# A fused attention and feed-forward layer on eight cores: the weights' fp32-to-bf16 conversion is moved from VectorE into the GpSimd-issued load

## The chip, the cores and the metric

The kernel runs on all 8 cores of one Trainium2 chip. Each core takes two of the sixteen sequences of the batch and all the weights; nothing is exchanged between cores. The metric is the device time in microseconds of the slowest core.

## What is computed

```
x = L0_attn_x                                  # 16 x 2048 x 1024, fp32
h = layernorm(x)
keys    = h @ triu(Wk).T                       # 16 heads of 64
queries = h @ tril(Wq).T
values  = h @ Wv.T
att = softmax(queries . keys / 8)              # per head, 2048 x 2048
x = x + layernorm((att . values) @ Wu.T + bu)
g = layernorm(x)
x = x + layernorm(g @ weight.T + pooled(g) @ disha)   # pooled: sum over 16 groups of 64 columns
```

Each layernorm is over the 1024 columns, with epsilon 1e-5 and no gain. All matrix products are done in bf16 with fp32 accumulation.

## The kernel before

One core works through its two sequences, b = 0 and b = 1, of 2048 rows each (16 blocks of 128 rows). There are five 1024x1024 fp32 weights in HBM. TensorE wants them in bf16 and transposed, so each is brought in by eight *preps*, one for each block of 128 rows (`prep_weight_thunks`, L232). A prep has these steps:

- SyncE (SP) issues the load of the fp32 rows into one of two staging tiles `wraw0`, `wraw1` (L245). A full block is 128x1024, 512 KB.
- VectorE casts them to the single bf16 tile `wc2` (L249).
- For Wk and Wq, which are triangular, only 1 to 8 of the 128-column groups are loaded. SP loads a 128x128 mask into the single tile `mkt0` (L253) and VectorE multiplies the diagonal group by it (L257).
- TensorE transposes each 128x128 group by a matmul with the identity into the PSUM tile `psO` (L262). Below, the up to 8 matmuls of one prep are called T.
- VectorE (in the first stage ScalarE) evacuates `psO` to the resident weight tile `slotA`, `slotB` or `slotC` (L278, L273).

`mini_prep_thunk` (L284) does the same for the first row block of Wk and of Wq into a tile `mini`, with L286 the load, L289 the cast, L293 and L296 the mask, L300 the transposes and L305 the evacuation.

Every engine runs its instructions in the order in which the Python code emits them. A small class `Prog` keeps, for each named region, the last writer and the readers since, and turns these into semaphore waits. A DMA is an instruction of the queue of the engine that issues it, and a waiting instruction holds up all behind it on that engine. A load into a tile waits for the last reader of what stood there.

The stages are, in order of time:

1. `ph1`, b = 0 only (0 to 176 us): layernorm and transposition of the 16 row blocks, with the 24 preps of Wk, Wq and Wv mixed in, three (Wk, Wq, Wv) in each of the first eight steps, and the first projections.
2. `ph2` (176 to 1025 us for b = 0, 1341 to 2150 us for b = 1): attention in 32 *units*. A unit is two heads by 512 queries, with 16 steps of two score matmuls (L499, L505), one exponential of 128x1024 on ScalarE (L511) and two matmuls with the values (L522, L528). The score matmuls of the next step are emitted ahead of the current step's value matmuls. At the end of each unit `emit_tail` (L535) inverts the row sums on ScalarE (L541, L543), sends them over HBM to be spread over 64 partitions (`rrd`, `rbsb`; L546, L548, L552), multiplies on VectorE (L557, L561), and moves one half to the upper partitions (L565). These four DMAs are issued by GpSimd (POOL). Behind the tails of units 26, 27, 28 and 29 stand four preps each, eight of Wu and then eight of the feed-forward weight. That is the case in both passes over `ph2`. Units 13 to 28 of b = 0 also carry the row statistics of b = 1 (`stats_thunks`), and the two mini preps stand behind the tail of unit 31 of b = 0.
3. `ph34` (1025 to 1297 us, 2150 to 2388 us): output projection, layernorms, feed-forward product and stores, as a software pipeline over the 16 row blocks. POOL issues its stores `xp` and `out` (L713, L776), SP its loads. At its end, for b = 0, stand the 16 preps of Wk and Wq for b = 1 (1297 to 1341 us).

So before, POOL's queue holds only the tails' DMAs and the stores, and all weight loads are on SP's queue, where the two staging tiles let it run up to two preps ahead.

Of the kernel before, what the change touches and what calls it, by code (L numbers as in the profile page):

```python
# [6 lines left out]
F32 = mybir.dt.float32  # L7
BF16 = mybir.dt.bfloat16
# [131 lines left out]
D = 1024  # L140
# [10 lines left out]
def build_nc():  # L151
# [16 lines left out]
    sb = lambda n, sh, dt: es.enter_context(nc.sbuf_tensor(n, sh, dt))  # L168
# [26 lines left out]
    onescf = sb("onescf", [1, 128], F32)  # L195
    ones128 = sb("ones128", [128, 1], BF16)
    idn = sb("idn_s", [128, 128], BF16)
    wraw = [sb("wraw0", [128, D], F32), sb("wraw1", [128, D], F32)]
    wc2 = sb("wc2", [128, D], BF16)
    mkt = [sb("mkt0", [128, D], BF16)] * 2  # L200
    dstg = jnk

    def make_fam(pfx):
# [7 lines left out]
    def fk(fam, n, j):  # L211
# [3 lines left out]
    psO = pst("psO")  # L215
# [3 lines left out]
    p = Prog()  # L219
# [6 lines left out]
         writes=["bub"], tag="bu_b16")  # L226
# [5 lines left out]
    def prep_weight_thunks(wd, slot_t, slot_key, mask_d, tagp, tri=None,  # L232
                           widx=0, evac_eng="dve"):
        ths = []
        for fb in range(NDC):
            def th(fb=fb):
                if tri == "low":
                    lo, hi = 0, fb + 1
                elif tri == "up":
                    lo, hi = fb, NDC  # L240
                else:
                    lo, hi = 0, NDC
                wr = wraw[(fb + widx) % 2]
                wrk = f"wraw{(fb + widx) % 2}"
                p.dma("sync", lambda e: e.dma_start(  # L245
                    wr[:, lo * 128:hi * 128],
                    wd[fb * 128:(fb + 1) * 128, lo * 128:hi * 128]),
                    writes=[wrk], tag=f"{tagp}_ld{fb}")
                p.op("dve", lambda e: e.tensor_copy(  # L249
                    wc2[:, lo * 128:hi * 128], wr[:, lo * 128:hi * 128]),  # L250
                    reads=[wrk], writes=["wc2"], tag=f"{tagp}_c{fb}")
                if mask_d is not None:
                    p.dma("sync", lambda e: e.dma_start(  # L253
                        mkt[0][:, 0:128],
                        mask_d[fb * 128:(fb + 1) * 128, fb * 128:(fb + 1) * 128]),
                        writes=["mkt0"], tag=f"{tagp}_ldm{fb}")
                    p.op("dve", lambda e: e.tensor_mul(  # L257
                        wc2[:, fb * 128:(fb + 1) * 128],
                        wc2[:, fb * 128:(fb + 1) * 128], mkt[0][:, 0:128]),
                        reads=["mkt0", "wc2"], writes=["wc2"], tag=f"{tagp}_m{fb}")  # L260
                for dc in range(lo, hi):
                    p.op("pe", lambda e, dc=dc: e.matmul(  # L262
                        psO[:, dc * 128:(dc + 1) * 128],
                        wc2[:, dc * 128:(dc + 1) * 128],
                        idn[:], start=True, stop=True),
                        reads=["wc2", "idn"], writes=["psO"],
                        tag=f"{tagp}_t{fb}_{dc}")
                sdst = lambda: slot_t[:].rearrange(
                    "p (dc f) -> p dc f", dc=NDC)[:, lo:hi, fb * 128:(fb + 1) * 128]
                ssrc = lambda: psO[:, :].rearrange(  # L270
                    "p (dc f) -> p dc f", dc=NDC)[:, lo:hi, :]
                if evac_eng == "act":
                    p.op("act", lambda e: e.activation(  # L273
                        sdst(), ssrc(), AF.Identity),
                        reads=["psO"], writes=[(slot_key, fb)],
                        tag=f"{tagp}_e{fb}")
                else:
                    p.op("dve", lambda e: e.tensor_copy(sdst(), ssrc()),  # L278
                         reads=["psO"], writes=[(slot_key, fb)],
                         tag=f"{tagp}_e{fb}")  # L280
            ths.append(th)
        return ths

    def mini_prep_thunk(wd, mask_d, base, mkey, tagp, ndc=NDC):  # L284
        def th():
            p.dma("sync", lambda e: e.dma_start(  # L286
                wraw[0][:, 0:ndc * 128], wd[0:128, 0:ndc * 128]),
                writes=["wraw0"], tag=f"{tagp}_ld")
            p.op("dve", lambda e: e.tensor_copy(  # L289
                wc2[:, 0:ndc * 128], wraw[0][:, 0:ndc * 128]),  # L290
                reads=["wraw0"], writes=["wc2"], tag=f"{tagp}_c")
            if mask_d is not None:
                p.dma("sync", lambda e: e.dma_start(  # L293
                    mkt[0][:, 0:128], mask_d[0:128, 0:128]), writes=["mkt0"],
                    tag=f"{tagp}_lm")
                p.op("dve", lambda e: e.tensor_mul(  # L296
                    wc2[:, 0:128], wc2[:, 0:128], mkt[0][:, 0:128]),
                    reads=["mkt0", "wc2"], writes=["wc2"], tag=f"{tagp}_m")
            for dc in range(ndc):
                p.op("pe", lambda e, dc=dc: e.matmul(  # L300
                    psO[:, dc * 128:(dc + 1) * 128],
                    wc2[:, dc * 128:(dc + 1) * 128],
                    idn[:], start=True, stop=True),
                    reads=["wc2", "idn"], writes=["psO"], tag=f"{tagp}_t{dc}")
            p.op("dve", lambda e: e.tensor_copy(  # L305
                mini[:, base:base + ndc * 128], psO[:, 0:ndc * 128]),
                reads=["psO"], writes=[mkey], tag=f"{tagp}_e")
        return th
# [629 lines left out]
```

How the kernel before makes its waits and increments, by code:

```python
                    def body(eng):  # L111
                        highwater = {}
                        for o in self.ops[eng_name]:
                            needed = {}
                            for prod in o.waits:
                                if prod not in sem_val_after:
                                    raise RuntimeError(
                                        f"dep of {o.tag} on {prod.tag} lost")
                                k, v = sem_val_after[prod]
                                if needed.get(k, 0) < v:
                                    needed[k] = v
                            for k, v in needed.items():
                                if highwater.get(k, 0) < v:
                                    eng.wait_ge(sems[k], v)
                                    highwater[k] = v
                            inst = o.fn(eng)
                            if o in sem_val_after:
                                k, _ = sem_val_after[o]
                                inst.then_inc(sems[k], 16 if o.is_dma else 1)
                        for k, v in counters.items():
                            if highwater.get(k, 0) < v:
                                eng.wait_ge(sems[k], v)
```

## Time and profile before

| | us |
|---|---|
| median of 2 runs | 2366.76 (2365.36 to 2368.15) |
| the profiled execution | 2389.16 |
| its span, core 0, the slowest | 2387.6 |
| spans of the eight cores | 2353.2 to 2387.6 |
| busy in the span: PE, ACT, DVE, POOL | 1705.7, 1502.0, 663.6, 167.5 |

The span runs from the first to the last instruction of the slowest core. PE is TensorE, ACT ScalarE, DVE VectorE, POOL GpSimd, SP SyncE. A POOL or SP row of a DMA is its issue; its data land later. The number in square brackets of a row is the time the engine sat idle before it, with what ended the wait. "x8" is a count of like instructions that were merged in one row.

### The profile page before, as it was taken

The page shows a single profiled execution, that of the slowest core. Times are in us where ns is not written, and L with a number is a line of the kernel's source. Part 1 is how long each engine was busy: PE and PEld are TensorE (multiplying, and loading weights), DVE is VectorE, ACT ScalarE, POOL GpSimd, SP SyncE. Part 2 cuts the span into 40 slices and gives each one's busy share as a digit, 9 for nine tenths or more (in the row PEclk, how much of TensorE's full clock was granted, in tenths as well). Part 3 has the DMA queues.
Part 4 walks back from the last instruction along what each step waited for, and adds up shares of the span by engine and source line. Part 5 has one row for each costly group of instructions (what it writes and reads, how often), then busy time and mean ns, then how long its engine had stood idle before and what let it go on. Part 6 is the DMA issues. An engine that isn't in the chain of part 4 may idle for free.

```text
span 2387.6 us, 28615 instructions; the slowest of 8 cores (2353.2 to 2387.6 us)
## 1 busy us (share of the span) xinstructions
PE 1705.7 (71%) x8793; PEld 625.6 (26%) x8793; DVE 663.6 (28%) x1515; ACT 1502.0 (63%) x1821; POOL 167.5 (7%) x324
## 2 busy tenths in 40 slices
PE   1358888888888654667774588888888884557773
PEld 1232322322323221123332132322322222112231
DVE  3441111122223231224454211111111113123544
ACT  3347777777778644536663377777787873555554
POOL 0000010000000100000000001010000100000000
PEclk9769877779989877778886699999899896779887
DMA  3320000000111021125554200000000002112443
GB/s 115 127 95 12 12 16 13 15 23 30 44 34 48 18 93 54 34 95 174 166 179 141 69 13 17 12 18 12 18 16 13 18 12 81 42 55 86 151 166 141
DMA packets 51590, 148.04 MB, mean 62 GB/s; under 512 B 14193, under 2 KB 15857, under 8 KB 51442
## 3 DMA queue, kind: packets, MB, share of 16 engines
q1 hardware_dynamic: 31986, 91.41, 12.0%
q0 software_dynamic: 19456, 54.81, 6.5%
q8 instruction: 75, 1.23, 0.2%
q14 instruction: 73, 0.60, 0.1%
HBM read 108.17 MB, written 33.82 MB: 59 GB/s over the span
## 4 chain that ended last, share of the span: by engine, by line
PE 48%; ACT 21%; issue 13%; DVE 11%; DMA 5%; ACTq 1%; DVEq 0%; SPq 0%; POOLq 0%; POOL 0%
ACT pt L511 11%; PE psS L499 11%; PE psO L522 5%; PE psM L522 5%; PE psO L528 4%; PE psM L423 4%; PE psM L528 4%; PE psM L454 3%; PE psO L423 3%; PE psO L454 3%; ACT fbuf L541 2%; PE psS L664 2%; PE psS L736 2%; PE psO L262 2%; DVE qf L438 2%
## 5 line engine op out<-in xcount | busy, mean ns | idle before, releaser
L511 ACT ACTIVATE pt<-psS 128x1024 bf16<-128x1024 f32 x1024 | 1031.8, 1024 | 514.8 <-PE psS L505 413.2
L505 PE MATMUL psS<-qf,kf 64*128 64x512 bf16 x1024 | 436.3, 426 | 0.0
L499 PE MATMUL psS<-qf,kf 64*128 64x512 bf16 x1024 | 436.3, 426 | 0.0
L522 PE MATMUL psO<-pt,vp 128*65 128x512 bf16 x512 | 221.2, 432 | 101.6 <-ACT pt L511 95.6
L522 PE MATMUL psM<-pt,vp 128*65 128x512 bf16 x512 | 214.3, 419 | 107.8 <-ACT pt L511 105.5
L262 PE MATMUL psO<-idn_s,wc 128*128 128x128 bf16 x464 | 60.9, 305 | 246.4 <-DVE wc L249 147.0
L499 PEld LDWEIGHTS psS<-qf,kf 64*128 64x128 bf16 x1024 | 95.8, 94 | 490.8 <-issue 490.7
L528 PE MATMUL psO<-pt,vp 128*65 128x512 bf16 x512 | 220.3, 430 | 0.0
L736 PE MATMUL psS<-slotB,lnxt 128*128 128x512 bf16 x512 | 156.5, 474 | 85.5 <-ACT lnxt L367 84.2
L528 PE MATMUL psM<-pt,vp 128*65 128x512 bf16 x512 | 213.5, 417 | 0.0
L664 PE MATMUL psS<-slotA,aofm 128*128 128x512 bf16 x512 | 127.4, 394 | 16.7 <-ACT psS L687 11.5
L546 POOL DMA_DIRECT2D rrd<-fbuf x64 | 32.3, 504 | 1392.0 <-ACT fbuf L543 1392.0
L557 DVE TENSOR_TENSOR aofm<-psO,rbsb 64x512 bf16<-64x512 f32 x32 | 21.9, 683 | 355.4 <-DMA rbsb<-rrd 299.6
L454 PE MATMUL psM<-slotC,lnxt 128*128 128x128 bf16 x1152 | 97.4, 232 | 31.1 <-DVE kf L438 17.8
L522 PEld LDWEIGHTS psO<-pt,vp 128*65 128x65 bf16 x512 | 59.2, 116 | 209.9 <-issue 202.5
L522 PEld LDWEIGHTS psM<-pt,vp 128*65 128x65 bf16 x512 | 58.4, 114 | 211.0 <-issue 203.6
L262 PEld LDWEIGHTS psO<-idn_s,wc 128*128 128x128 bf16 x464 | 44.1, 135 | 264.6 <-issue 264.6
L557 DVE TENSOR_TENSOR aofm<-psM,rbsb 64x512 bf16<-64x512 f32 x32 | 21.9, 683 | 324.8 <-DMA rbsb<-rrd 254.4
L736 PEld LDWEIGHTS psS<-slotB,lnxt 128*128 128x128 bf16 x512 | 57.7, 117 | 174.5 <-issue 145.2
L505 PEld LDWEIGHTS psS<-qf,kf 64*128 64x128 bf16 x1024 | 95.9, 94 | 0.0
L465 DVE CAST vp<-psM 128x128 bf16<-128x128 f32 x144 | 42.3, 294 | 177.2 <-PE psM L454 168.2
L454 PEld LDWEIGHTS psM<-slotC,lnxt 128*128 128x128 bf16 x1152 | 72.2, 104 | 63.2 <-issue 63.2
(114 smaller groups left out, 1878.4 us busy)
## 6 DMA issues: line engine op xcount, KB each, us to landing
xt<-x SPq DMA_DIRECT2D x64, 512.0 KB, 4.2
rbsb<-rrd POOLq DMA_DIRECT2D x128, 128.0 KB, 2.9
xp<-xt POOLq DMA_DIRECT2D x32, 512.0 KB, 3.5
xt<-xp SPq DMA_DIRECT2D x32, 512.0 KB, 3.6
out<-xt POOLq DMA_DIRECT2D x32, 512.0 KB, 2.9
wraw<-wu SPq DMA_DIRECT2D x16, 512.0 KB, 4.2
wraw<-wf SPq DMA_DIRECT2D x16, 512.0 KB, 4.1
fbuf<-x SPq DMA_DIRECT2D x16, 512.0 KB, 5.3
```

What stands on the lines that cost most here:

```text
L262: p.op("pe", lambda e, dc=dc: e.matmul(psO[:, dc * 128:(dc + 1) * 128], wc2[:, dc * 128:(dc + 1) * 128], idn[:], start=True, stop=True), r ...
L423: slot_t=slot_t, half=half: e.matmul(ps[:, qtr * 512:(qtr + 1) * 512], slot_t[:, colf(dc):colf(dc) + 128], lnxt[:, dc * T + (half * 2 + qt ...
L438: p.op("dve", lambda e: e.tensor_copy(dst_t[:, (half * 2 + qtr) * 512:(half * 2 + qtr) * 512 + 512], ps[:, qtr * 512:(qtr + 1) * 512]), re ...
L454: p.op("pe", lambda e, tcl=tcl, tc=tc, dc=dc, ps=ps: e.matmul(ps[:, tcl * 128:(tcl + 1) * 128], lnxt[:, dc * T + tc * 128:dc * T + (tc + 1 ...
L499: p.op("pe", lambda e: e.matmul(psS[sp][:, 0:512], kf[par][0:64, kc * 128:(kc + 1) * 128], qf[par][0:64, q0:q0 + 512], start=True, stop=Tr ...
L505: p.op("pe", lambda e: e.matmul(psS[sp][:, 512:1024], kf[par][64:128, kc * 128:(kc + 1) * 128], qf[par][64:128, q0:q0 + 512], start=True, ...
L511: p.op("act", lambda e: e.activation(pt[sp][:, :], psS[sp][:, :], AF.Exp, scale=SCALE), reads=[PSS[sp]], writes=[f"pt{sp}"], tag=f"u{uidx} ...
L522: p.op("pe", lambda e: e.matmul(psA[0:65, 0:512], vp[par][:, kc * 130:kc * 130 + 65], pt[sp][:, 0:512], start=(kc == 0), stop=(kc == KCN - 1),
L528: p.op("pe", lambda e: e.matmul(psA[0:65, 512:1024], vp[par][:, kc * 130 + 65:kc * 130 + 130], pt[sp][:, 512:1024], start=(kc == 0), stop= ...
L541: p.op("act", lambda e: e.activation(fbuf[0][64:65, :], psA[64:65, :], AF.Ln), reads=[psk], writes=["fbuf0"], tag=f"u{uidx}rc1")
L664: p.op("pe", lambda e, half=half, ec=ec: e.matmul(psS[0][:, half * 512:(half + 1) * 512], aofm[:, ec * T + tc * 128:ec * T + (tc + 1) * 12 ...
L736: p.op("pe", lambda e, half=half, dc=dc: e.matmul(psS[1][:, half * 512:(half + 1) * 512], lnxt[:, dc * T + tc * 128:dc * T + (tc + 1) * 12 ...
```

## The change

The fp32 staging tiles and the cast are taken away. POOL issues the weight load straight into a bf16 tile, and the DMA converts from fp32 to bf16. There are now two bf16 tiles (`wc2a`, `wc2b`), used in turn, and two mask tiles, used in turn. The mini preps use the first tile of each kind only. The masks stay on SP's queue. The row blocks, the matmuls, the evacuations and the order of all on PE and ACT are the same. A line number of after is 1 to 4 lower than that of before for the same statement.

```diff
-    wraw = [sb("wraw0", [128, D], F32), sb("wraw1", [128, D], F32)]
-    wc2 = sb("wc2", [128, D], BF16)
-    mkt = [sb("mkt0", [128, D], BF16)] * 2
+    wcp = [sb("wc2a", [128, D], BF16), sb("wc2b", [128, D], BF16)]
+    wc2 = wcp[0]
+    mkt = [sb("mkt0", [128, 128], BF16), sb("mkt1", [128, 128], BF16)]
...
-                wr = wraw[(fb + widx) % 2]
-                wrk = f"wraw{(fb + widx) % 2}"
-                p.dma("sync", lambda e: e.dma_start(
-                    wr[:, lo * 128:hi * 128],
+                wi = (fb + widx) % 2
+                wc = wcp[wi]
+                wck = f"wc2{wi}"
+                p.dma("pool", lambda e: e.dma_start(
+                    wc[:, lo * 128:hi * 128],
                     wd[fb * 128:(fb + 1) * 128, lo * 128:hi * 128]),
-                    writes=[wrk], tag=f"{tagp}_ld{fb}")
-                p.op("dve", lambda e: e.tensor_copy(
-                    wc2[:, lo * 128:hi * 128], wr[:, lo * 128:hi * 128]),
-                    reads=[wrk], writes=["wc2"], tag=f"{tagp}_c{fb}")
+                    writes=[wck], tag=f"{tagp}_ld{fb}")
...
     def mini_prep_thunk(wd, mask_d, base, mkey, tagp, ndc=NDC):
         def th():
-            p.dma("sync", lambda e: e.dma_start(
-                wraw[0][:, 0:ndc * 128], wd[0:128, 0:ndc * 128]),
-                writes=["wraw0"], tag=f"{tagp}_ld")
-            p.op("dve", lambda e: e.tensor_copy(
-                wc2[:, 0:ndc * 128], wraw[0][:, 0:ndc * 128]),
-                reads=["wraw0"], writes=["wc2"], tag=f"{tagp}_c")
+            p.dma("pool", lambda e: e.dma_start(
+                wc2[:, 0:ndc * 128], wd[0:128, 0:ndc * 128]),
+                writes=["wc20"], tag=f"{tagp}_ld")
```

The mask multiply, the transposes and the mask load follow the tile by its key (`wck`, `mkt{wi}`).

What this does to the order shows best at the end of a unit that has preps. Before, POOL's queue at the end of unit 26 of b = 0 is the tail's four DMAs (`rrd`, `rbsb` twice, `aofm`), and then the next unit's:

```order
L546 DMA rrd<-fbuf0 16x1x64
L548 DMA rbsb<-rrd 64x512
L552 DMA rbsb<-rrd 64x512
L565 DMA aofm<-stg2 64x512
L546 DMA rrd<-fbuf0 16x1x64
```

After, the four loads of Wu's row blocks stand between the two:

```order
L542 DMA rrd<-fbuf0 16x1x64
L544 DMA rbsb<-rrd 64x512
L548 DMA rbsb<-rrd 64x512
L561 DMA aofm<-stg2 64x512
L246 DMA wc2a<-wu 128x1024
L246 DMA wc2b<-wu 128x1024
L246 DMA wc2a<-wu 128x1024
L246 DMA wc2b<-wu 128x1024
L542 DMA rrd<-fbuf0 16x1x64
```

The loads have moved from SP's queue, where nothing but other weight loads and the statistics' `xt` loads stood ahead of them, to behind `aofm<-stg2`.

On VectorE the same place reads, before, with the casts between the tail's two multiplies (L557, L561), the evacuations to `slotA` and the statistics (L577, L580):

```order
L557 TENSOR_TENSOR aofm<-psO,rbsb 64x512
L561 TENSOR_TENSOR stg2<-psO,rbsb 64x512
L249 CAST wc2<-wraw0 128x1024
L278 CAST slotA<-psO 128x8x128
L249 CAST wc2<-wraw1 128x1024
L278 CAST slotA<-psO 128x8x128
L249 CAST wc2<-wraw0 128x1024
L278 CAST slotA<-psO 128x8x128
L249 CAST wc2<-wraw1 128x1024
L278 CAST slotA<-psO 128x8x128
L577 TENSOR_REDUCE sxal<-xt1 128x1
```

and after:

```order
L553 TENSOR_TENSOR aofm<-psO,rbsb 64x512
L557 TENSOR_TENSOR stg2<-psO,rbsb 64x512
L277 CAST slotA<-psO 128x8x128 x4
L573 TENSOR_REDUCE sxal<-xt1 128x1
L576 SCALAR_TENSOR_TENSOR jnk,sqal<-xt1 128x1024
```

The casts are gone and nothing takes their place. The third place is POOL's queue at the end of unit 31 of b = 0, ahead of the first stores `xp` of `ph34`. After, the loads of the two mini preps stand there, both into `wc2a`, behind the tail's last DMA:

```order
L542 DMA rrd<-fbuf0 16x1x64
L544 DMA rbsb<-rrd 64x512
L548 DMA rbsb<-rrd 64x512
L561 DMA aofm<-stg2 64x512
L285 DMA wc2a<-wk 128x1024
L285 DMA wc2a<-wq 128x128
L709 DMA xp<-xt0 128x1024
```

Before, L713, the `xp` store, followed L565 directly there.

## Rows read from the trace of the kernel before

**Rows 1.** The page's costliest groups: the transposes of the preps.
```profile
L262 PE MATMUL psO<-idn_s,wc 128*128 128x128 bf16 x464 | 60.9, 305 | 246.4 <-DVE wc L249 147.0
```
**Rows 2.** Timeline, end of unit 26 of b = 0: start us, us, engine, instruction.
```profile
832.19 0.68 DVE L561 TENSOR_TENSOR stg<-psO,rbsb 64x512 bf16<-64x512 f32 x1
832.79 0.68 DVE L249 CAST wc<-wraw 128x1024 bf16<-128x1024 f32 x1
833.44 0.52 POOL L565 DMA_DIRECT2D aofm<-stg  x1 [4.01 <-DVE stg L561]
...
833.72 1.01 PE L262 MATMUL psO<-idn_s,wc 128*128 128x128 bf16 x8 [10.65 <-DVE wc L249]
834.84 1.23 DVE L278 CAST slotA<-psO 128x1024 bf16<-128x1024 f32 x1 [1.37 <-PE psO L262]
...
842.99 1.01 PE L262 MATMUL psO<-idn_s,wc 128*128 128x128 bf16 x8 [2.08 <-DVE wc L249]
843.93 0.60 PE L499 MATMUL psS<-qf,kf 64*128 64x512 bf16 x1
...
844.66 1.02 ACT L511 ACTIVATE pt<-psS 128x1024 bf16<-128x1024 f32 x1 [19.00 <-PE psS L505]
```
**Rows 3.** Timeline, end of unit 29 of b = 1, the last of the eight.
```profile
2097.54 0.67 DVE L561 TENSOR_TENSOR stg<-psM,rbsb 64x512 bf16<-64x512 f32 x1
...
2109.18 0.60 PE L499 MATMUL psS<-qf,kf 64*128 64x512 bf16 x1
```
**Rows 4.** DMA issues of the whole run: count, KB each, median us to landing.
```profile
out<-xt POOLq DMA_DIRECT2D x32, 512.0 KB, 2.9
wraw<-wu SPq DMA_DIRECT2D x16, 512.0 KB, 4.2
...
aofm<-stg POOLq DMA_DIRECT2D x64, 64.0 KB, 1.9
```
**Rows 5.** Tile wraw, 820 to 1020 us.
```profile
DMA to landing us min/median/max: 3.6/4.6/5.5
```
**Rows 6.** Line L713, the stores xp.
```profile
DMA to landing us min/median/max: 2.9/3.5/7.1
```
**Rows 7.** Tile wraw: the casts, ns min/median/max.
```profile
L249 DVE CAST wc<-wraw x72: 216/680/695, 20.1 to 2107.4; 128x1024 bf16<-128x1024 f32 x44, 128x128 bf16<-128x128 f32 x4, 128x896 bf16<-128x896 f32 x4, 128x256 bf16<-128x256 f32 x4
```
**Rows 8.** Timeline, the first two steps of ph1.
```profile
21.38 1.01 PE L262 MATMUL psO<-idn_s,wc 128*128 128x128 bf16 x8 [21.38 <-DVE wc L257]
21.63 0.38 SPq L245 DMA_DIRECT2D wraw<-wv  x1
...
25.24 0.27 PE L262 MATMUL psO<-idn_s,wc 128*128 128x128 bf16 x1 [2.85 <-DVE wc L257]
...
27.14 1.01 PE L262 MATMUL psO<-idn_s,wc 128*128 128x128 bf16 x8 [1.64 <-DVE wc L249]
...
34.55 0.90 PE L262 MATMUL psO<-idn_s,wc 128*128 128x128 bf16 x7 [2.99 <-DVE wc L257]
...
39.90 1.01 PE L262 MATMUL psO<-idn_s,wc 128*128 128x128 bf16 x8 [1.49 <-DVE wc L249]
```
**Rows 9.** Timeline, the 16 preps between the sequences: the first and the last.
```profile
1289.74 0.53 POOL L776 DMA_DIRECT2D out<-xt  x1 [9.49 <-DVE vp L465]
...
1297.79 0.22 DVE L257 TENSOR_TENSOR wc<-wc,mkt 128x128 bf16<-128x128 bf16 x1
...
1298.16 1.01 PE L262 MATMUL psO<-idn_s,wc 128*128 128x128 bf16 x8 [1.47 <-DVE wc L257]
...
1340.18 1.01 PE L262 MATMUL psO<-idn_s,wc 128*128 128x128 bf16 x8 [2.64 <-DVE wc L257]
```
**Rows 10.** Timeline, the mini preps at the end of unit 31 of b = 0.
```profile
1020.57 0.52 POOL L565 DMA_DIRECT2D aofm<-stg  x1 [3.92 <-DVE stg L561]
...
1021.08 1.01 PE L300 MATMUL psO<-idn_s,wc 128*128 128x128 bf16 x8 [11.35 <-DVE wc L296]
...
1025.31 0.26 PE L300 MATMUL psO<-idn_s,wc 128*128 128x128 bf16 x1 [3.23 <-DVE wc L296]
```

More of the change, by code:

```diff
@@ L242, in th @@
                     lo, hi = 0, NDC
-                wr = wraw[(fb + widx) % 2]
-                wrk = f"wraw{(fb + widx) % 2}"
-                p.dma("sync", lambda e: e.dma_start(
-                    wr[:, lo * 128:hi * 128],
+                wi = (fb + widx) % 2
[3 more added lines that the diff above has]
+                    wc[:, lo * 128:hi * 128],
                     wd[fb * 128:(fb + 1) * 128, lo * 128:hi * 128]),
-                    writes=[wrk], tag=f"{tagp}_ld{fb}")
-                p.op("dve", lambda e: e.tensor_copy(
-                    wc2[:, lo * 128:hi * 128], wr[:, lo * 128:hi * 128]),
-                    reads=[wrk], writes=["wc2"], tag=f"{tagp}_c{fb}")
+                    writes=[wck], tag=f"{tagp}_ld{fb}")
                 if mask_d is not None:
                     p.dma("sync", lambda e: e.dma_start(
-                        mkt[0][:, 0:128],
+                        mkt[wi][:, 0:128],
                         mask_d[fb * 128:(fb + 1) * 128, fb * 128:(fb + 1) * 128]),
-                        writes=["mkt0"], tag=f"{tagp}_ldm{fb}")
+                        writes=[f"mkt{wi}"], tag=f"{tagp}_ldm{fb}")
                     p.op("dve", lambda e: e.tensor_mul(
-                        wc2[:, fb * 128:(fb + 1) * 128],
-                        wc2[:, fb * 128:(fb + 1) * 128], mkt[0][:, 0:128]),
-                        reads=["mkt0", "wc2"], writes=["wc2"], tag=f"{tagp}_m{fb}")
+                        wc[:, fb * 128:(fb + 1) * 128],
+                        wc[:, fb * 128:(fb + 1) * 128], mkt[wi][:, 0:128]),
+                        reads=[f"mkt{wi}", wck], writes=[wck],
+                        tag=f"{tagp}_m{fb}")
                 for dc in range(lo, hi):
@@ L263, in th @@
                         psO[:, dc * 128:(dc + 1) * 128],
-                        wc2[:, dc * 128:(dc + 1) * 128],
+                        wc[:, dc * 128:(dc + 1) * 128],
                         idn[:], start=True, stop=True),
-                        reads=["wc2", "idn"], writes=["psO"],
+                        reads=[wck, "idn"], writes=["psO"],
                         tag=f"{tagp}_t{fb}_{dc}")
@@ L297, in th @@
                     wc2[:, 0:128], wc2[:, 0:128], mkt[0][:, 0:128]),
-                    reads=["mkt0", "wc2"], writes=["wc2"], tag=f"{tagp}_m")
+                    reads=["mkt0", "wc20"], writes=["wc20"], tag=f"{tagp}_m")
             for dc in range(ndc):
@@ L303, in th @@
                     idn[:], start=True, stop=True),
-                    reads=["wc2", "idn"], writes=["psO"], tag=f"{tagp}_t{dc}")
+                    reads=["wc20", "idn"], writes=["psO"], tag=f"{tagp}_t{dc}")
             p.op("dve", lambda e: e.tensor_copy(
```

## The prediction

> **What bounds the kernel now.** I read the page's groups first, for the instructions that the change touches. The transposes of the preps are 61 us of TensorE's work, yet TensorE sat idle 246.4 us before them, and 147.0 us of that ended on the cast [rows 1]. So the preps are made of waits, and the question is what each wait consists of and what comes last once the cast is gone. The timeline answers it, place by place. There are four places.
>
> The first is the end of a unit that carries preps [rows 2]. TensorE takes its work in order, so the score matmul of the next unit (L499) stands behind four T. VectorE ends the tail's last multiply at 832.87 (832.19 + 0.68) and casts at once, because the fp32 rows were already there: SP had loaded them long before. T starts at 833.72, the fourth at 842.99, and L499 at 843.93. ScalarE, which carries the exponentials, was idle 19.00 us. From the multiply's end to L499 it is 11.06 us. At the last of the eight such unit ends it is 2109.18 - 2098.21 = 10.97 us [rows 3]. Nothing covers this time, so each microsecond added or taken here is a microsecond of the span.
>
> The others are the first eight steps of ph1 [rows 8], the 16 preps between the sequences [rows 9], and the two mini preps [rows 10]. The attention units without preps and ph34 proper hold no prep, and I count nothing there.
>
> **The unknown: the converting load.** No row shows a DMA that converts. I call L its time from issue to landing for 512 KB of fp32. The nearest rows are POOL's stores of the same bytes, 2.9 us [rows 4], SP's weight loads over the run, 4.2 [rows 4], SP's weight loads in the stage with the preps, 3.6 to 5.5 with a median of 4.6 [rows 5], and POOL's slowest `xp` store, 7.1 [rows 6]. I take 4.4, between the two medians of loads of the same rows, and keep 2.9 and 7.1 as the ends. For 64 KB I take 2.5, somewhat over POOL's 1.9 for 64 KB within SBUF [rows 4]. By these two points a block of k groups takes 2.23 + 0.27k.
>
> **Unit ends, eight times.** What goes is the cast, 0.68 us, four times. What comes is that the loads stand on POOL behind `aofm<-stg`, which waits for the tail's multiply. The prefetch is lost altogether: the tiles are free, but the queue is not. Count from the multiply's end. POOL starts `aofm<-stg` 0.57 later (833.44 - 832.87) and is done at 1.09. Load 1 lands at 1.09 + L and T1 starts 0.1 later. T1 takes 1.01, its evacuation 1.23 with 0.11 ahead of it, so T2 starts 2.45 after T1 and ends at 4.65 + L. Load 4 goes into the tile that T2 read. It is issued 0.57 later (the same delay of POOL), lands L later, and T4 takes 0.1 + 1.01 more: 6.33 + 2L. Load 3 with T3 and its evacuation lets T4 start at the same time. Against 11.0 before, the difference is 2L - 4.7, which is +4.1 at L = 4.4. Eight times that is **+32.8**. Two load times are exposed where there were none, and the four casts don't pay for them. Break-even is L = 2.35, below every row of this size.
>
> **ph1, eight steps.** The pace of a step is set by Wv: before, SP issues its load 0.25 after T of Wk starts (21.63 against 21.38), since the cast had freed the staging tile. T of Wv starts 5.76 and 5.35 us after T of Wk in the two steps shown [rows 8], 5.55 in the mean. After, that load waits until T of Wk has ended: 0.64 (mean of 1.01 for eight groups and 0.27 for one) + 0.57 + 4.4 + 0.1 = 5.71, so +0.15. The cast of Wk ahead of its T also goes: it lies between 0.68 for eight groups and 0.22 for one, 0.45 in the mean [rows 7]. Net -0.3 a step, **-2.4**. The cast of Wv lay inside the 5.55. The mask wait of Wq goes too, but Wv is later anyway, so it is worth nothing.
>
> **Preps between the sequences.** Before, the first T starts at 1298.16 and the last ends at 1341.19 [rows 9]. POOL's last `out` store is issued at 1289.74, so loads 1 and 2 follow it and have landed before VectorE gets there. The first T starts 0.7 earlier (no cast), at 1297.5, and the second near 1300.1. From there every load waits for the T two before it. A pair costs T 0.64 + 0.57 + load 3.35 (mean of the seven blocks, 4.1 groups) + mask multiply 0.22 and its handovers 0.15, 4.93 in all. Seven pairs are 34.5: the last T starts at 1334.6 and ends at 1335.6, **-5.6**.
>
> **Mini preps.** Before, both were ready at once, T starting at 1021.08 and 1025.31 [rows 10]. After, the load of Wk follows `aofm<-stg` on POOL at 1021.09, so its T starts at 1021.09 + 4.4 + 0.1 + 0.37 = 1025.96, +4.9. The second load goes into the same tile and waits for the first T: 1.01 + 0.57 + 2.5 + 0.47 = 4.55 against 4.23 before, +0.3. Together **+5.2**. The first output projection waits behind them on TensorE.
>
> **Sum.** 32.8 - 2.4 - 5.6 + 5.2 = +30.0 us. The profiled execution took 2389.16 us (span 2387.6), 0.95% over the median of the runs. The unit ends are waits on DMA and VectorE, alike on any core, so I add the same microseconds to the median: 2366.76 + 30.0 = 2396.8, +1.3%. By the profiled execution it is 2419.2. Per microsecond of L the sum moves by 16 + 8 + 7 + 2 = 33 us.
>
> **Rivals.** *The converting load is quick.* At L = 2.9, POOL's time for the same bytes outward, the unit ends cost 1.1 each (+8.8), ph1 gives back 14.4, the preps between the sequences some 14 (there the chain of T, evacuation and multiply then holds), and the minis cost 2.2: 2349 us, -0.7%. For it speaks that POOL's rows are shorter than SP's. Against it, a store is no load from HBM, and two loads are in flight together. The Trainium skill, in "DMA: Bandwidth & Descriptors", section "Anatomy of one DMA — SWDGE (gpsimd) path", gives for a DMA issued from GpSimd a fixed 2.0 us plus its bytes at 436 GB/s. For 512 KB that is an estimate of 3.2 us, and by it the sum would be 9.6 us below before, 2357. This case's `out` row agrees with it roughly, SP's loads do not.
>
> *The converting load is slow.* The conversion is work that no DMA here does yet, and it is exposed twice at each unit end and once in every ph1 step. At L = 7.1 the sum is 8 x 9.5 + 19.2 + 13.3 + 10.6 = +119, 2486 us. The place is the unit end, the price 16 us of the span per microsecond of L there, and from L = 4.9 on the kernel is slower by over 2% (47 us). Against it speaks that the write into SBUF is half as long and POOL's issue takes the 0.52 us of any other. The Trainium skill, in "SBUF — State Buffer", section "SBUF: two separate sides", warns that a DMA issued from GpSimd can stall when VectorE runs a fast-mode copy, as its descriptors can't be written meanwhile. The same change takes those casts away, so by that rule this rival gets weaker; no row here shows such a stall.
>
> *POOL's queue delays the tails or stores.* A load waiting for a T would hold up the next unit's `rrd` store. But the fourth load is issued before T4, and `rrd` comes a whole unit later. The stores of ph34 have no load ahead of them but the minis'. I give it no price and count it in the chances above.
>
> **How the numbers follow.** Forecast 48% (L from 3.8 to 4.9), quick load 20%, slow load 32%. Low end: L = 3.2, 2357. High end: L = 6, 30 + 53 = +83, 2450. Beyond them I leave about a tenth on either side. Faster by over 2%, about what a measurement of this kernel can tell from no change, would need more than all that the quick case gives: 2%. Slower by over 2% is the slow case, 32%. Within 2%: 66%.
>
> **What would show it.** In the profile after: look at the landing time of `wc<-wu` on POOL's queue (4.4), at the time from the tail's multiply to L499 at unit 26 (15.1 instead of 11.06) with ScalarE idle some 23 us, at T of Wv 5.7 us behind T of Wk in ph1, at 38 us instead of 43 for the preps between the sequences, and at the first mini T 5 us later behind the tail's multiply. TensorE's wait before T should end on a DMA where it ended on the cast. I am wrong if the loads at unit ends are issued ahead of `aofm<-stg`, if L is outside 3.8 to 4.9, or if the units without preps change their length.

## The result, and the profile after

After takes 2406.53 us (median of 9 runs, 2402.91 to 2443.79), before 2366.19 (8 runs, 2360.06 to 2400.14). The ratio is 1.0171, with a 95% interval of 1.0157 to 1.0185: slower by 1.7%, clear of the noise but within the 2% that counts as no change. The forecast was 2396.8, +30.0 us; measured it is +40.3. Some executions of either kernel fall into a slower state, in which one die is granted a lower clock (the 2443.79 is one), and every ratio here leaves those out.

First the page's groups of after: the transposes of the preps, now one group for each bf16 tile.

```profile
L261 PE MATMUL psO<-idn_s,wc2a 128*128 128x128 bf16 x236 | 30.9, 306 | 211.6 <-DMA wc2a<-wu 75.4
L261 PE MATMUL psO<-idn_s,wc2b 128*128 128x128 bf16 x228 | 30.0, 305 | 72.6 <-DMA wc2b<-wv 18.1
```

TensorE's work is the same 61 us. Its idle time before them has grown from 246.4 us [rows 1] to 284.2, and it ends on a DMA where it ended on VectorE's cast. VectorE's busy time fell from 663.6 to 625.7 us. The 38 us fewer of VectorE's work did not shorten the program.

The timeline at the end of unit 26 of b = 0, core 3, to be laid beside [rows 2]:

```profile
802.55 1.05 ACT L539 ACTIVATE fbuf<-fbuf 1x1024 f32<-1x1024 f32 x1
807.08 0.50 POOL L542 DMA_DIRECT2D rrd<-fbuf  x1 [17.96 <-issue]
...
813.96 0.67 DVE L557 TENSOR_TENSOR stg<-psO,rbsb 64x512 bf16<-64x512 f32 x1
815.20 0.52 POOL L561 DMA_DIRECT2D aofm<-stg  x1 [4.88 <-DVE stg L557]
815.71 0.57 POOL L246 DMA_DIRECT2D wc2a<-wu  x1
816.27 0.56 POOL L246 DMA_DIRECT2D wc2b<-wu  x1
820.15 1.01 PE L261 MATMUL psO<-idn_s,wc2a 128*128 128x128 bf16 x8 [19.14 <-DMA wc2a<-wu]
...
821.70 0.53 POOL L246 DMA_DIRECT2D wc2a<-wu  x1 [4.87 <-PE psO L261]
822.64 1.01 PE L261 MATMUL psO<-idn_s,wc2b 128*128 128x128 bf16 x8 [1.48 <-DVE slotA L277]
824.19 0.53 POOL L246 DMA_DIRECT2D wc2b<-wu  x1 [1.96 <-PE psO L261]
825.88 1.01 PE L261 MATMUL psO<-idn_s,wc2a 128*128 128x128 bf16 x8 [2.23 <-DMA wc2a<-wu]
828.39 1.01 PE L261 MATMUL psO<-idn_s,wc2b 128*128 128x128 bf16 x8 [1.50 <-DVE slotA L277]
829.34 0.60 PE L495 MATMUL psS<-qf,kf 64*128 64x512 bf16 x1
...
830.07 1.02 ACT L507 ACTIVATE pt<-psS 128x1024 bf16<-128x1024 f32 x1 [26.47 <-PE psS L501]
```

Read it from the multiply's end, 814.63. The loads stand behind `aofm<-stg`. The first T waits for a load, the third T waits for another, and the score matmul L495 comes 14.71 us after the multiply, where it came 11.06 us after it in before. There is one thing more, in the first two rows, that nothing in the forecast had. ACT ends L539 at 803.60, and POOL issues `rrd` 3.48 us later, after 17.96 us of idle time that ended on nothing the profile shows. Over the eight unit ends the time from the multiply to the score matmul is 14.7 to 15.3 us (medians over the cores), where before has 11.0 to 11.3.

The DMA issues of after. The KB are those written, so 256.0 stands for 512 KB read; the last number is the median from issue to landing:

```profile
wc2a<-wu POOLq DMA_DIRECT2D x8, 256.0 KB, 4.0
wc2b<-wu POOLq DMA_DIRECT2D x8, 256.0 KB, 4.5
...
wc2a<-wv POOLq DMA_DIRECT2D x4, 256.0 KB, 4.3
wc2b<-wv POOLq DMA_DIRECT2D x4, 256.0 KB, 5.1
```

In [rows 4] SP's fp32 load of `wu` took 4.2. In the stage with the preps, 820 to 1020 us, line L246 of after shows:

```profile
DMA to landing us min/median/max: 3.7/4.1/4.8
```

Rows say where a wait is, not how much it adds up to. So here is the time by stage, from the trace's records: for each core from the start of one exponential of ScalarE, or one T, to that of the next stage, and then the median over the eight cores of the profiled execution. (`ph34` of b = 1 and the mini preps are counted from the end of the last exponential ahead of them, the minis up to the end of their last T.) Medians don't add up exactly, and `ph1` with the same code came out between 175.6 and 178.9 in three kernels, so a difference of 3 us there says nothing.

| us | before | after |
|---|---|---|
| `ph1` | 175.2 | 175.6 |
| unit end 26, b = 0 | 41.3 | 48.3 |
| the other seven unit ends with preps | 287.2 | 312.8 |
| mini preps | 15.7 | 24.7 |
| preps between the sequences | 41.7 | 42.1 |
| `ph34` of b = 1, to the end | 239.2 | 234.8 |
| of that, last `out` issue to the end | 10.09 | 6.62 |
| whole span | 2355.4 | 2397.6 |

The stage of a unit end is the unit behind it: from its first exponential, which still runs ahead of the T, to the first one of the next unit. The units without preps agree within 1 us per 13 units. So the loss is at the unit ends, +32.6, and at the minis, +9.0. `ph1` and the preps between the sequences have gained nothing. The end of the program has given back 3.5.

The minis, core 3, against [rows 10]:

```profile
1018.03 0.52 POOL L561 DMA_DIRECT2D aofm<-stg  x1 [3.97 <-DVE stg L557]
1018.54 0.57 POOL L285 DMA_DIRECT2D wc2a<-wk  x1
...
1024.13 1.01 PE L296 MATMUL psO<-idn_s,wc2a 128*128 128x128 bf16 x8 [16.46 <-DVE wc2a L292]
1024.49 1.31 SPq L692 DMA_DIRECT2D xt<-x  x3
...
1025.70 0.54 POOL L285 DMA_DIRECT2D wc2a<-wq  x1 [6.58 <-PE psO L296]
1025.96 0.33 SPq L779 DMA_DIRECT2D fbuf<-x  x1
1032.13 0.23 DVE L292 TENSOR_TENSOR wc2a<-wc2a,mkt 128x128 bf16<-128x128 bf16 x1 [5.66 <-DMA wc2a<-wq]
```

The second load writes only 32 KB, and yet the multiply that waits for it comes 6.43 us after its issue. Beside it run four 512 KB loads that SP has just issued (L692, three of them, and L779).

### The profile page after: what moved, and what is told of

Same layout as the page of the kernel before. It is cut to its first block, busy times and chain, and to the rows that moved or that the text cites. A ratio compares the mean times of both kernels' runs of the same rounds, so it can differ in the third digit from the quotient of the medians.

```text
span 2405.5 us, 28454 instructions; the slowest of 8 cores (2387.3 to 2405.5 us)
## 1 busy us (share of the span) xinstructions
PE 1673.4 (70%) x8793; PEld 621.8 (26%) x8793; DVE 625.7 (26%) x1441; ACT 1496.8 (62%) x1821; POOL 206.3 (9%) x398
## 4 chain that ended last, share of the span: by engine, by line
PE 45%; ACT 22%; issue 13%; DVE 10%; DMA 8%; ACTq 1%; DVEq 0%; POOL 0%; POOLq 0%; SPq 0%
ACT pt L507 12%; PE psS L495 10%; PE psO L518 5%; PE psM L518 5%; PE psM L419 4%; PE psO L524 4%; PE psM L524 3%; PE psM L450 3%; PE psO L419 3%; ACT fbuf L537 3%; PE psO L450 2%; PE psS L660 2%; PE psO L261 2%; DVE qf L434 2%; PE psS L732 2%
## 5 line engine op out<-in xcount | busy, mean ns | idle before, releaser
L495 PE MATMUL psS<-qf,kf 64*128 64x512 bf16 x1024 | 425.8, 416 | 0.0
L501 PE MATMUL psS<-qf,kf 64*128 64x512 bf16 x1024 | 425.8, 416 | 0.0
L518 PE MATMUL psO<-pt,vp 128*65 128x512 bf16 x512 | 213.4, 417 | 108.5 <-ACT pt L507 101.9
L518 PE MATMUL psM<-pt,vp 128*65 128x512 bf16 x512 | 209.8, 410 | 108.7 <-ACT pt L507 105.1
L495 PEld LDWEIGHTS psS<-qf,kf 64*128 64x128 bf16 x1024 | 95.4, 93 | 472.0 <-issue 472.0
L524 PE MATMUL psO<-pt,vp 128*65 128x512 bf16 x512 | 212.4, 415 | 0.0
L524 PE MATMUL psM<-pt,vp 128*65 128x512 bf16 x512 | 209.7, 410 | 0.0
L261 PE MATMUL psO<-idn_s,wc2a 128*128 128x128 bf16 x236 | 30.9, 306 | 211.6 <-DMA wc2a<-wu 75.4
L261 PE MATMUL psO<-idn_s,wc2b 128*128 128x128 bf16 x228 | 30.0, 305 | 72.6 <-DMA wc2b<-wv 18.1
## 6 DMA issues: line engine op xcount, KB each, us to landing
wc2a<-wu POOLq DMA_DIRECT2D x8, 256.0 KB, 4.0
```

Of the source, the lines that this page charges most:

```text
L261: p.op("pe", lambda e, dc=dc: e.matmul(psO[:, dc * 128:(dc + 1) * 128], wc[:, dc * 128:(dc + 1) * 128], idn[:], start=True, stop=True), re ...
L495: p.op("pe", lambda e: e.matmul(psS[sp][:, 0:512], kf[par][0:64, kc * 128:(kc + 1) * 128], qf[par][0:64, q0:q0 + 512], start=True, stop=Tr ...
L501: p.op("pe", lambda e: e.matmul(psS[sp][:, 512:1024], kf[par][64:128, kc * 128:(kc + 1) * 128], qf[par][64:128, q0:q0 + 512], start=True, ...
L518: p.op("pe", lambda e: e.matmul(psA[0:65, 0:512], vp[par][:, kc * 130:kc * 130 + 65], pt[sp][:, 0:512], start=(kc == 0), stop=(kc == KCN - 1),
L524: p.op("pe", lambda e: e.matmul(psA[0:65, 512:1024], vp[par][:, kc * 130 + 65:kc * 130 + 130], pt[sp][:, 512:1024], start=(kc == 0), stop= ...
```

## The experiments

**One, the queue without the conversion.** Before, with its fp32 tiles and its casts, but the weight loads issued by POOL:

```diff
-                p.dma("sync", lambda e: e.dma_start(
+                p.dma("pool", lambda e: e.dma_start(
                     wr[:, lo * 128:hi * 128],
...
-            p.dma("sync", lambda e: e.dma_start(
+            p.dma("pool", lambda e: e.dma_start(
                 wraw[0][:, 0:ndc * 128], wd[0:128, 0:ndc * 128]),
```

> The kernel before, with nothing changed but the queue that issues the fp32 weight loads: GpSimd instead of SyncE. VectorE still casts. Theory (the lost prefetch): at each of the eight unit ends the first load is issued only behind aofm<-stg, 1.09 us after the tail's multiply, so the first T starts one load time later; the later loads are released by the casts and hide behind the chain of evacuation, cast and T. Unit ends 1.1 + 4.1 = 5.2 us longer each, 42 us in all, the mini preps some 6 us longer, ph1 and the preps between the sequences within 2 us of before: about 2414 us. Rival (the conversion in the DMA is what is slow, and the queue position costs little): a POOL load of fp32 lands like SP's and the unit ends stay within 1 us of before: 2366 to 2376 us.

Measured: 2424.19 us, ratio 1.0247 (1.0225 to 1.0269). The unit ends cost +43.8 us against before, where 42 was expected. `ph1` cost +7.3 and the preps between the sequences +5.0, where at most 2 was expected for each; those two mostly explain the 10 us by which the kernel is slower than foreseen. Nothing converts here, and the kernel is slower than after. Its loads, by the DMA issues of the run:

```profile
wraw<-wu POOLq DMA_DIRECT2D x16, 512.0 KB, 4.1
...
wraw<-wv POOLq DMA_DIRECT2D x8, 512.0 KB, 5.2
```

Laid beside the rows of after, they show that the conversion costs little or nothing: 4.1 without it, 4.0 and 4.5 with it. (The converting load also writes half the bytes, so a small cost of the conversion and a small gain by the bytes could hide each other; no run tells them apart.) What costs at the unit ends is the place in POOL's queue. In `ph1`, where `wv` is on the path, POOL's loads of it take 5.2 without the conversion and 4.3 and 5.1 with it (after), and SP's 4.0 in the fourth experiment. Why POOL's are longer there isn't shown.

**Two, the prefetch restored.** After, with the first two loads of each group of four issued four steps ahead of the unit's end, before the tail's DMAs:

```diff
+            if kc == KCN - 4:
+                due = [th for mu, th in bpreps if mu <= uidx
+                       and hasattr(th, "pre")][:2]
+                for th in due:
+                    th.pre()
             emit_av(b, uidx, kc)
```

> The changed kernel, with the first two loads of each group of four preps issued four steps ahead of the end of the unit, in front of the tail's DMAs in GpSimd's queue. Theory (the lost prefetch): the first two T start as soon as the tail's multiply lets them, loads 3 and 4 are each exposed in part only, and the multiply-to-L499 time is about 9.4 us after even units and 8.8 after odd ones, where before had 11.0 and the changed kernel about 14.7 to 15: some 48 us less than the changed kernel, about 2358 us. Rival (the converting load is slow by itself): loads 3 and 4 still cost a full load time each beyond that and only half of the 33 us comes back, about 2390 us.

Measured: 2356.56 us, ratio 0.9955 (0.9940 to 0.9970). The unit ends are 16.5 us below before in sum, where after was 32.6 above. The timeline of unit 26 of b = 0, core 4:

```profile
788.72 0.52 POOL L574 DMA_DIRECT2D aofm<-stg  x1 [4.01 <-PE psS L514]
792.16 0.57 POOL L249 DMA_DIRECT2D wc2a<-wu  x1 [2.92 <-PE psS L514]
...
810.26 0.68 DVE L570 TENSOR_TENSOR stg<-psO,rbsb 64x512 bf16<-64x512 f32 x1 [0.31 <-DMA rbsb<-rrd]
811.09 1.01 PE L268 MATMUL psO<-idn_s,wc2a 128*128 128x128 bf16 x8 [10.19 <-DVE stg L570]
...
812.65 0.57 POOL L249 DMA_DIRECT2D wc2a<-wu  x1 [0.62 <-PE psO L268]
...
816.86 1.01 PE L268 MATMUL psO<-idn_s,wc2a 128*128 128x128 bf16 x8 [2.27 <-DMA wc2a<-wu]
...
820.75 0.60 PE L508 MATMUL psS<-qf,kf 64*128 64x512 bf16 x1
```

T1 now waits for the tail's multiply and starts 0.15 us behind it. One load is still exposed, the one before T3. L508 comes 9.81 us after the multiply, below the 11.06 of before. So with the casts gone and half of the prefetch kept the change is a small gain. The rows also put the wait of 2.92 us that ends at 792.16 on POOL. The profile names a matmul as its end, but that had been done for long; experiment seven says what it is.

**Three, more tiles in place of an earlier issue.** After, with four bf16 tiles used in turn and nothing moved:

```diff
-    wcp = [sb("wc2a", [128, D], BF16), sb("wc2b", [128, D], BF16)]
+    wcp = [sb(f"wc2{c}", [128, D], BF16) for c in "abcd"]
...
-                wi = (fb + widx) % 2
+                wi = rot[0] % 4
+                rot[0] += 1
```

> The changed kernel with four bf16 weight tiles used in turn instead of two, nothing moved. Theory: no load waits for a T any more, except in the minis. Unit ends still wait for the first load behind aofm<-stg but for one load only: 13.7 us instead of about 15, 12 us less over the eight. In ph1 the load of Wv is issued before T of Wk and steps get 2 us shorter, 16 in all; the preps between the sequences become a chain of T and evacuation and lose about 10. About 2368 us. Rival (the converting loads are bound by the rate at which they convert): four in flight each take longer, the unit ends and ph1 stay as they are, 2400 us or more.

Measured: 2367.79 us, ratio 1.0003 (0.9981 to 1.0026). The sum comes out as expected, but less of it from the unit ends: they are still 24.1 us above before, 8.5 better than after where 12 was expected. `ph1` went from 175.6 to 153.5 and the preps between the sequences from 42.1 to 33.0. At a unit end the first load is exposed whatever the depth, and with four loads in flight each takes longer from issue to landing than the one before it:

```profile
wc2a<-wu POOLq DMA_DIRECT2D x4, 256.0 KB, 4.0
...
wc2d<-wu POOLq DMA_DIRECT2D x4, 256.0 KB, 6.6
```

**Four, the masks alone.** Before, with nothing changed but the second mask tile:

```diff
-    mkt = [sb("mkt0", [128, D], BF16)] * 2
+    mkt = [sb("mkt0", [128, 128], BF16), sb("mkt1", [128, 128], BF16)]
...
+                mi = (fb + widx) % 2
```

> The kernel before, with nothing of the change but its two mask tiles instead of one. Theory: in the preps between the sequences VectorE waited 8.4 us in nine waits for a mask; these go, so that stage takes 33 us instead of 42, and nothing else moves, since in ph1 the mask wait lies beside the load of Wv: 2358 us. If so, the converting loads cost that stage what the masks gave it. Rival: the masks are hidden there too behind the chain of evacuations, and the time stays 2366 us.

Measured: 2355.24 us, ratio 0.9967 (0.9937 to 0.9997). `ph1` 168.2 instead of 175.2, where nothing was expected; the preps between the sequences 36.6 instead of 41.7, where 9 us less was expected (the 8.4 us of waits for a mask were core 0's; over the cores it is 4.7 to 8.7). The rest is as before. The timeline of the first step of `ph1`, core 0, beside [rows 8], which is the same core:

```profile
18.65 0.33 SPq L246 DMA_DIRECT2D wraw<-wv  x1
...
19.15 1.01 PE L263 MATMUL psO<-idn_s,wc 128*128 128x128 bf16 x8 [19.15 <-DVE wc L258]
...
23.24 1.01 PE L263 MATMUL psO<-idn_s,wc 128*128 128x128 bf16 x8 [1.54 <-DVE wc L250]
```

T of Wv comes 4.09 us behind T of Wk instead of 5.76. In before, Wv's load stood on SP's queue behind the mask's load, which waited for the multiply that used the only mask tile. With two mask tiles Wv's load leaves right after the cast, at 18.65.

So the change was two changes, a queue and a second mask tile. In `ph1` the masks alone give 7.0 us and the queue alone takes 7.3 (experiment one), and after has +0.4. That looks like a sum and isn't one. Once Wv's load is on POOL's queue, no mask stands ahead of it any more. In experiment one, core 2, it is issued 0.03 us ahead of T of Wk (18.82), and T of Wv, at 25.03, is late because the load takes 5.2:

```profile
18.79 0.53 POOL L245 DMA_DIRECT2D wraw<-wv  x1 [15.98 <-DVE wc L257]
```

In after, core 3, the same load waits for T of Wk to have read the tile:

```profile
19.86 1.01 PE L261 MATMUL psO<-idn_s,wc2a 128*128 128x128 bf16 x8 [19.86 <-DVE wc2b L255]
...
21.41 0.53 POOL L246 DMA_DIRECT2D wc2a<-wv  x1 [18.62 <-DVE fasx L340]
...
27.50 1.01 PE L261 MATMUL psO<-idn_s,wc2a 128*128 128x128 bf16 x8 [5.09 <-DMA wc2a<-wv]
```

From the start of one T to that of the next, mean over the steps of `ph1`, medians over the cores:

| us | before | masks (four) | POOL (one) | after |
|---|---|---|---|---|
| Wk to Wq | 2.63 | 1.87 | 2.42 | 1.53 |
| Wk to Wv | 5.41 | 4.47 | 6.43 | 5.96 |
| Wv to the next Wk | 8.13 | 8.13 | 8.13 | 7.65 |

In after T of Wq comes 1.1 us sooner, and T of Wv doesn't: it waits for its load. The last row is the cast of Wk, which only after is without. Between the sequences -5.1 for the masks and +5.0 for POOL aren't parts of after's +0.4 either, as experiment six shows. What the second mask tile is worth in after itself no run here shows.

**Five, all of it.** After, with four weight tiles, all four loads of a group issued four steps ahead, and the minis' loads and masks issued in the same way into tiles of their own:

```diff
-    wcp = [sb("wc2a", [128, D], BF16), sb("wc2b", [128, D], BF16)]
+    wcp = [sb(f"wc2{c}", [128, D], BF16) for c in "abcd"]
...
+            if kc == KCN - 4:
+                due = [th for mu, th in bpreps if mu <= uidx
+                       and hasattr(th, "pre")][:4]
+                for th in due:
+                    th.pre()
+                    del th.pre
             emit_av(b, uidx, kc)
```

> After, with four bf16 weight tiles, two mask tiles, all four loads of a group issued four steps before the end of its unit, ahead of the tail's DMAs, and the loads of the two minis issued in the same way into tiles of their own. Theory (what costs is the loads' place on POOL's queue and the depth of the buffers, the conversion nothing): the eight unit ends each end 2.5 us earlier than before the change (-20 in all, where the version with two hoisted loads gave -16.5), ph1 as with four tiles (-22), the preps between the sequences some 33 us (-9), the minis some 2 us below before, the program's end -3.5: 2366 - 56 = about 2312 us, 2.3% faster than before. Rival (four loads of 512 KB in flight delay rrd, rbsb and each other, so that the tails grow by what the preps lose): unit ends no better than before, 2330 us or more.

Measured: 2303.66 us, ratio 0.9734 (0.9709 to 0.9759), faster than before by 2.7%. The unit ends are 26.6 us below before, `ph1` 154.4, the preps between the sequences 31.9, the minis 15.1. The tails did not grow: from the start of the tail's L543 (or its counterpart) to that of the multiply L561 it is 7.3 to 7.5 us at all eight ends, in before 7.3 to 7.7. Core 6, unit 26 of b = 0:

```profile
788.32 0.67 DVE L588 TENSOR_TENSOR stg<-psO,rbsb 64x512 bf16<-64x512 f32 x1
789.14 1.01 PE L274 MATMUL psO<-idn_s,wc2a 128*128 128x128 bf16 x8 [9.67 <-DVE stg L588]
...
796.61 1.01 PE L274 MATMUL psO<-idn_s,wc2d 128*128 128x128 bf16 x8 [1.48 <-DVE slotA L290]
```

T1 waits for the tail's multiply, T2 to T4 for the evacuation ahead of each, and no T for a load. What is left is T and its evacuation, 2.49 us a prep; from the multiply to the end of T4 it is 8.63 us, where it was 11.13 in before (842.99 + 1.01 - 832.87). The expectation was 8 us too high, 6.6 of it at the unit ends: T3 no longer waits for its load either.

**Six, SP held back.** After, but the first three `xt` loads of `ph34` wait for the last mini, or for the last prep of Wq:

```diff
+            hold = ["miniQ" if b == 0 else ("slotB", 7)] if tc < 3 else []
...
-                writes=[xkey], tag=f"p3b{b}_ld{tc}")
+                reads=hold, writes=[xkey], tag=f"p3b{b}_ld{tc}")
```

> After, but the first three row-block loads of ph34 on SP's queue wait until the second mini prep is done (b = 0), or until the last prep of Wq is done (b = 1). Theory (the mini's second load took 6.3 us and the last prep's load 7.7 us because SP, which no longer stands behind weight loads, issues its 512 KB row-block loads beside them): these two loads fall to 2.5 to 3.5 and 4.4 us, the minis' stage from 24.7 to about 21, the preps between the sequences from 42.1 to about 39, the program to about 2400 us. What the held row blocks may cost at the start of ph34 counts against it. Rival (the two loads are slow for another reason): both stages as in after, 2406 us.

Measured: 2397.48 us, ratio 1.0117 (1.0082 to 1.0152). The minis' stage fell from 24.7 to 20.4, the preps between the sequences from 42.1 to 37.9. Core 3:

```profile
1024.97 0.54 POOL L285 DMA_DIRECT2D wc2a<-wq  x1 [5.57 <-PE psO L296]
1028.22 0.22 DVE L292 TENSOR_TENSOR wc2a<-wc2a,mkt 128x128 bf16<-128x128 bf16 x1 [2.47 <-DMA wc2a<-wq]
...
1029.37 1.27 SPq L693 DMA_DIRECT2D xt<-x  x3
```

The small load is there after 3.25 us where it took 6.43. Holding back big loads that nobody waits for yet was worth 4.3 + 4.2 = 8.5 us, and `ph34` of b = 0 became no longer by it.

**Seven, one DMA more on POOL.** The late `rrd` in after, 4.53 us after the start of L539 instead of 1.60, stands at the same place on all eight cores, and in experiments one, three and six as well. It is POOL's 129th DMA each time. After, with a single DMA moved:

```diff
-    p.dma("sync", lambda e: e.dma_start(idn[:], idn_d), writes=["idn"], tag="ld_idn")
+    p.dma("pool", lambda e: e.dma_start(idn[:], idn_d), writes=["idn"], tag="ld_idn")
```

> After, with the load of the identity (the first DMA of the program) issued by POOL instead of SP, so that every later DMA of POOL stands one place further on in its queue. In after the 129th DMA of POOL, which is rrd of unit 26 of b = 0, is issued 4.53 us after the start of the logarithm's follower (L539) on every core, and every other rrd 1.60 us; in before the 129th is a store of ph34. Theory (POOL pauses for some 2.9 us at its 129th DMA, whatever that DMA is): rrd of unit 26 is issued after 1.6 us, the pause falls on the aofm DMA of unit 25, which carries no preps and hides it, the first unit end with preps falls from 48.3 to 45.4 us and the program by about 3 us. Rival (the pause belongs to that unit or to the first load of Wu behind it): 4.53 us and 48.3 us stay.

Measured: 2399.36 us, ratio 1.0112 (1.0025 to 1.0200), 7 us below after's median, though the interval is too wide to make much of that. The stage is sharp: 45.1 instead of 48.3. The timeline of POOL, core 0:

```profile
790.06 0.52 POOL L561 DMA_DIRECT2D aofm<-stg  x1 [6.73 <-issue]
802.64 0.50 POOL L542 DMA_DIRECT2D rrd<-fbuf  x1 [12.07 <-ACT fbuf L539]
```

The unexplained wait has moved to `aofm` of unit 25, issued 4.18 us after the start of its multiply instead of 1.25. `rrd` of unit 26 waits for ACT again.

**Eight, sixty DMAs more on POOL.** Before, with sixty loads of 8 bytes added on POOL's queue, two a unit in the attention of b = 1 (work added, none left out):

```diff
+            if b == 1 and uidx < 30 and kc in (4, 5):
+                k = 2 * uidx + kc - 4
+                p.dma("pool", lambda e, k=k: e.dma_start(
+                    dum[:, k * 4:(k + 1) * 4], idn_d[0:1, 0:4]),
+                    writes=[f"dum{k}"], tag=f"dum{k}")
```

> Before, with sixty further loads of 8 bytes into a tile of their own, issued by POOL two a unit in units 0 to 29 of b = 1, so that POOL issues 380 DMAs instead of 320; the weight loads stay on SP. From the issue of the last store to the end of the span it was 10.05 us in before and 6.6 in after (394 POOL DMAs), with POOL's last DRAIN 6.5 against 2.8. Theory (the length of the final drain goes by how many DMAs POOL has issued since its last pause, and the pauses come at the 129th, the 250th and so every 121 DMAs, next at the 371st): 6.6 us or less from the last store to the end. Rival (it goes by where the weight loads are issued, SP or POOL): 10.05 us as before. Outside the end nothing moves by more than 1 us.

Measured: two runs, 2365.52 and 2422.32, which give no verdict on the time; the profile gives one on the end. On core 2, with a span of 2364.0, the last store is issued at:

```profile
2358.63 0.53 POOL L782 DMA_DIRECT2D out<-xt  x1 [6.24 <-DVE xt L778]
```

That is 5.35 us before the end (median of the cores 5.36), where before has 10.09. The weight loads are still SP's, so it isn't they. Ahead of the end no unit end moved by over 0.4 us, and no stretch of 13 units without preps by over 1.5, more than the 1 us that was expected.

## Why the prediction was right, and where not

**The unit ends: the mechanism is right, and the size too, but that by luck: two errors cancel.** The forecast was +4.1 an end at a load of 4.4 us. The load took 4.1, which by its formula, 2L - 4.7, gives 3.5; the seven ends cost 25.6 / 7 = 3.7 each. The first end cost 7.0, of which 2.93 is the pause of POOL. So 29.7 for the loads and 2.9 for the pause make 32.6, beside a forecast of 32.8. At unit 26 the forecast was 15.1 us from the multiply to L499 and it is 14.71 to its counterpart L495. ScalarE's idle time of 26.47 against some 23 is the pause, which lies ahead of the multiply. The fourth T waits for the evacuation ahead of it and the third for load 3, one of the two paths that the forecast had ending together. That the queue's place is the cause, and not the conversion, is shown twice: without conversion the loss is there (one), and with the loads ahead of the tail it turns into a gain (two).

**The unknown L.** The quick rival (2.9) and the slow one (7.1) both fell by the row 3.7/4.1/4.8. The Trainium skill, in "DMA: Bandwidth & Descriptors", section "Anatomy of one DMA — SWDGE (gpsimd) path", gave an estimate of 3.2 us for 512 KB; the trace doesn't agree, 4.1 in the median, with eight cores loading at the same points. The Trainium skill says in the same page, section "SWDGE vs HWDGE vs iDMA", that only a DMA issued from GpSimd can cast on its way. No run here tries it from another queue; by that rule the change had to move the loads to POOL's queue, and the cost at the unit ends came with the move.

**`ph1`: -2.4 forecast, +0.4 measured, a term mis-sized.** By the table of experiment four the wait for Wv grew from 5.41 to 5.96 us a step, +0.55, where the sum had 5.55 to 5.71, +0.15. The 5.55 was the mean of two steps on one core, and the load of Wv was taken as 4.4: it took 4.6 in the mean over the cores, 4.9 on core 3, with 6.9 in its second step. The other term holds: the cast of Wk was priced at 0.45 a step, and the way from Wv to the next Wk fell by 0.48. One reading was wrong without touching the sum. What let Wv's load go in before was not the cast but the mask's load ahead of it on SP, as experiment four shows. So a second mask tile is worth 7.0 us as long as the loads are SP's. In after T of Wv waits for its load, which no mask holds up, as the forecast had it ("Wv is later anyway"). The forecast didn't see the 7.0 that before left lying, which a change of the mask tile alone would have got.

**Preps between the sequences: -5.6 forecast, +0.4 measured.** The chain was priced without what SP would do once it was free of weight loads. It issues three `xt` loads of 512 KB into the last preps, and the last load of Wq took 7.7 us:

```profile
1336.36 1.32 SPq L692 DMA_DIRECT2D xt<-x  x3
...
1337.33 0.53 POOL L246 DMA_DIRECT2D wc2b<-wq  x1 [1.73 <-PE psO L261]
...
1345.10 0.23 DVE L255 TENSOR_TENSOR wc2b<-wc2b,mkt 128x128 bf16<-128x128 bf16 x1 [3.66 <-DMA wc2b<-wq]
```

With SP held back it is -3.8 (six), so this explains 4.2 of the 6.0 us. Most of the rest is the core that was read: the profile shown of before is core 0's, whose stage is 43.7 us by the measure of the table, and the median over the cores is 41.7.

**Minis: +5.2 forecast, +9.0 measured,** mostly by the same omission: the second load was priced at 2.5 us beside an idle SP. With SP held back the stage is +4.7.

**The end of the program: not foreseen,** 3.5 us given back. So 30.0 forecast stands against 40.3 measured. By stages: unit ends -0.2, `ph1` +2.8, preps +6.0, minis +3.8, the end -3.5 beside the forecast, 8.9 in all; the last 1.4 lie in the units without preps and in the medians.

**The rival of POOL's queue** ("a load waiting for a T would hold up the next `rrd`") didn't come about: away from the pause, `rrd` is issued 1.60 us after the start of L539, as in before.

## What to carry to other kernels

A load that is moved to another engine's queue takes that queue's waits, and the prefetch is lost even though its tile is free: emit the load ahead of whatever waits there. Before crediting a removed copy, ask what it hides behind; here a unit end lost 4.1 us (0.4 of it the pause) with no load early, and gained 2.1 with two and 3.3 with four. And price what the relieved queue will now do: SP's early 512 KB loads cost two loads on the path 3.2 us each (6.43 against 3.25, 7.7 against 4.5).

## What was not expected of the hardware

- **POOL pauses for 2.9 us by the count of its DMAs.** In all ten kernels, on every core, the 129th and the 250th are late, and so is the 371st in the eight kernels that issue so many: 121 apart. The 129th is `rrd` of unit 26 in four kernels and the first hoisted load in experiments two and five, and it moved with the count in seven. In before it is the first `xp` of `ph34`. The 250th is `rbsb` of unit 54 in before and `aofm` of unit 39 in after, the 371st in after a store `xp`, issued 3.54 us after the end of the instruction that it waits for (L704), where the stores `xp` have 0.57 in the median (core 3):

```profile
2253.63 0.53 POOL L709 DMA_DIRECT2D xp<-xt  x1 [4.50 <-issue]
```

  It cost 3.2 us at the unit end with preps (48.3 against 45.1 in seven); the units behind the late DMAs of units 39 and 54 are no longer than others. What is done in the pause isn't shown.
- **The end of the program goes by the same count.** The DRAIN that stands last on POOL's queue but for two semaphore instructions lasts 6.44 us with 320 DMAs (before), 2.60 with 394, 2.68 with 395 and 1.45 with 380, on every core. Counted from the last late DMA on, itself included, these are 71, 24, 25 and 10 DMAs, and 0.64 us + 0.082 for each fits all four. The form of that line is drawn from these four points alone.
- A load that converts 512 KB of fp32 took no longer than one that doesn't, on the same queue (4.0 and 4.5 us against 4.1), with half the bytes written.
